# Front attention: a new order on TensorE, VectorE and ScalarE, and two more copies on VectorE

## What is computed

```python
    scores = jnp.einsum('bhid,bhjd->bhij', q, k)
    rel = jnp.einsum('bhid,pd->bhip', q, rel_key)
    rel_idx = jnp.clip(j - i + p - 1, 0, p - 1)
    bias = jnp.take_along_axis(rel, rel_idx, axis=3)
    logits = jnp.where(j <= i, (scores + bias) * scale, -jnp.inf)
    attn = jax.nn.softmax(logits, axis=-1)
    out = jnp.einsum('bhij,bhjd->bhid', attn, v)
    return out.transpose(0, 2, 1, 3).reshape(b, s, e) @ Wo + bo
```

## Time and profile before

| | |
|---|---|
| median of 3 runs | 4286.01 us (4283.55 to 4286.08) |
| span of the profiled execution | 4281.5 us, 4.5 us under the median |
| TensorE matmul busy | 4088.3 us (95%) |
| TensorE weight load busy | 2939.1 us (69%) |
| VectorE busy | 3495.0 us (82%) |
| ScalarE busy | 3716.8 us (87%) |
| GpSimd busy | 2399.2 us (56%) |
| DMA, share of 16 engines | 26.8% over the span, 0.74 in the front attention |

### The profile page before, as it was taken

One profiled execution on the slowest core, in us unless ns is written; L12 is line 12 of the kernel. 1 busy time (PEld: TensorE's weight loads), 2 busy tenths in 40 slices (PEclk: granted clock), 3 DMA queues, 4 the chain that ended last, 5 costly groups with the idle time before them and its releaser, 6 DMA issues. The chain is left out here.

```text
span 4281.5 us, 124222 instructions
## 1 busy us (share of the span) xinstructions
PE 4088.3 (95%) x43826; PEld 2939.1 (69%) x43826; DVE 3495.0 (82%) x8236; ACT 3716.8 (87%) x7186; POOL 2399.2 (56%) x2876
## 2 busy tenths in 40 slices
PE   4999999987999999999999999999999999999995
PEld 2566666654777777777777777777777777777774
DVE  4788888866888888888888888888888888888884
ACT  4899999966998989989999899998999989999895
POOL 4000000026667776777777777777777777767763
PEclk7999999988999999999999999999999999999997
DMA  6777777741111111111111111111111111111111
GB/s 180 229 230 228 235 226 237 224 142 35 44 42 42 47 36 44 42 42 47 37 43 43 42 47 37 41 45 42 47 37 43 43 42 47 37 43 42 42 47 52
DMA packets 249884, 347.65 MB, mean 81 GB/s; under 512 B 45120, under 2 KB 206508, under 8 KB 249260
## 3 DMA queue, kind: packets, MB, share of 16 engines
q1 hardware_dynamic: 249388, 341.00, 26.8%
HBM read 151.13 MB, written 82.85 MB: 55 GB/s over the span
## 5 line engine op out<-in xcount | busy, mean ns | idle before, releaser
L1468 PE MATMUL la_ps<-la_Wqkv,la_xsT 128*128 128x512 f32 x2304 | 1181.3, 608 | 5.5 <-DVE X L1173 5.5
L1173 DVE TENSOR_TENSOR X<-la_ps,la_tab 128x1024 f32<-128x1024 f32 x768 | 934.3, 1217 | 116.8 <-ACT la_sq L1317 107.7
L1120 POOL TENSOR_TENSOR la_rt<-la_rt,la_rn 128x1024 f32<-128x1024 f32 x384 | 722.4, 1902 | 27.5
L1103 POOL TENSOR_TENSOR la_rt<-X 128x512 f32<-128x512 f32 x384 | 494.7, 1288 | 319.1 <-PE la_ps L1483 243.3
L1505 PEld LDWEIGHTS la_ps<-la_kT,la_qB 128*64 128x64 f32 x12288 | 389.3, 138 | 230.2 <-issue 218.8
L1180 DVE TENSOR_REDUCE la_ssum<-la_sq 128x8 f32<-128x512 f32 x768 | 503.2, 676 | 0.0
L1104 POOL TENSOR_TENSOR la_rt<-X 128x512 f32<-128x512 f32 x384 | 497.3, 1295 | 0.0
L1317 ACT ACTIVATE la_sq<-la_ps 128x512 f32<-128x512 f32 x768 | 457.7, 596 | 15.5 <-PE la_ps L1468 5.4
L1468 PEld LDWEIGHTS la_ps<-la_Wqkv,la_xsT 128*128 128x128 f32 x2304 | 377.9, 191 | 132.9 <-issue 93.5
L526 POOL COPY at_vh<-V 128x64 f32 (+1 forms) x64 | 15.1, 236 | 784.3 <-PE at_ps L725 783.2
L1505 PE MATMUL la_ps<-la_kT,la_qB 128*64 128x64 f32 x12288 | 442.4, 225 | 0.2 <-ACT la_kT L1349 0.2
(11 more groups left out here) (207 smaller groups left out, 9544.0 us busy)
## 6 DMA issues: line engine op xcount, KB each, us to landing
at_band<-skew_scratch SPq DMA_DIRECT2D x64, 1536.0 KB, 7.3
la_vs<-la_v SPq DMA_DIRECT2D x192, 384.0 KB, 3.5
skew_scratch<-at_R SPq DMA_DIRECT2D x64, 1024.0 KB, 6.6
la_vs<-la_v SPq DMA_DIRECT2D x192, 128.0 KB, 3.4
la_Wqkv<-in_wqkv SPq DMA_DIRECT2D x28, 384.0 KB, 4.7
at_qh<-qt_scratch SPq DMA_DIRECT2D x64, 144.0 KB
at_kh<-kt_scratch SPq DMA_DIRECT2D x64, 144.0 KB
la_W<-in_L_ffn_W SPq DMA_DIRECT2D x24, 341.0 KB, 4.5
```

The lines of the kernel that those rows point to most:

```text
L1103: e.tensor_tensor(dst[:, :, 0, :], c[:, :, 0, :], s[:, :, 1, :], ALU.add)
L1120: e.tensor_tensor(heads(rt, w), heads(rt, w), wide(rn[:, w * H:(w + 1) * H], D), ALU.mult)\
L1173: e.tensor_tensor(dst.rearrange("p f (h d) -> p f h d", d=D), ps[:, c % 2, :].rearrange("p (h d) -> p h d", d=D).unsqueeze(1).to_broadcast ...
L1468: e.matmul(ps[:, c % 2, :], xsT[:, m * P:(m + 1) * P], Wqkv[:, ds(layer(n) % 2, 1), c * 512:(c + 1) * 512], start=True, stop=True)\
```

## The change

`BY_DVE` grows from (3, 6, 10) to (2, 3, 6, 8, 10): VectorE copies turned blocks 2 and 8 too, which ScalarE did. The bodies of the three engines are reordered. The steps themselves, their waits, and SyncE's and GpSimd's programs don't change. On TensorE turns, scores and values are mixed more finely; between rel(n, 0) and scores(7) of head n-3 now stand turn 8, turn 9, values 1 and turn 10 of head n-4, scores 6 of n-3, turn 11 of n-4, rel(n, 1) and turn 0 of n-3. scores 2 and 3, turn 4 and values 0 move from the end of a round to the start of the next. On VectorE far_least(4) and drain(0) go to the start of the next round, drain(1) goes behind minimum 7, and over_sum(1) behind minima 0 and 1 of the next head. On ScalarE the round begins with rel(0)'s copy.

```diff
--- before.py
+++ after.py
@@ -40,7 +40,7 @@
 QKV_Q = 3 * INNER // LOADS
 RING_V, RING_T = 4, 4
 DEEPEST = 7
-BY_DVE = (3, 6, 10)
+BY_DVE = (2, 3, 6, 8, 10)
 DEEPEST_A = 4
 
 
@@ -578,35 +578,41 @@
 
             def body(t):
                 for n, m in t.back(4):
+                    drain(n, m, 0)
                     copied(n, m, 6)
+                for n, m in t.back(3):
+                    far_least(n, m, 4)
+                    least(n, m, 4)
+                for n, m in t.back(4):
                     over_sum(n, m, 0)
                 for n, m in t.back(3):
-                    least(n, m, 4)
                     far_least(n, m, 5)
+                for n, m in t.back(4):
+                    copied(n, m, 8)
+                for n, m in t.back(3):
                     least(n, m, 5)
                 for n, m in t.back(4):
                     copied(n, m, 10)
                 for n, m in t.back(3):
                     far_least(n, m, 6)
                     least(n, m, 6)
-                for n, m in t.back(4):
-                    drain(n, m, 1)
-                for n, m in t.back(3):
                     far_least(n, m, 7)
                     least(n, m, 7)
                 for n, m in t.back(4):
+                    drain(n, m, 1)
+                for n, m in t.back(2):
+                    least(n, m, 0)
+                for n, m in t.back(3):
+                    copied(n, m, 2)
+                for n, m in t.back(2):
+                    least(n, m, 1)
+                for n, m in t.back(3):
+                    copied(n, m, 3)
+                for n, m in t.back(4):
                     over_sum(n, m, 1)
-                for n, m in t.back(3):
-                    copied(n, m, 3)
-                for n, m in t.back(2):
-                    least(n, m, 0)
-                    least(n, m, 1)
+                for n, m in t.back(2):
+                    far_least(n, m, 3)
                     least(n, m, 2)
-                    far_least(n, m, 3)
-                for n, m in t.back(3):
-                    drain(n, m, 0)
-                for n, m in t.back(2):
-                    far_least(n, m, 4)
                     least(n, m, 3)
             rounds(e, body, HEADS_A, RING_A, DEEPEST_A)
 
@@ -637,42 +643,41 @@
                 e.activation(dst, src, ACT.Copy).then_inc(tA.sem, 1)
 
             def body(t):
-                for n, m in t.back(3):
-                    exp(n, m, 3)
-                for n, m in t.back(4):
-                    copied(n, m, 8)
-                    copied(n, m, 9)
-                for n, m in t.back(3):
-                    exp(n, m, 4)
-                for n, m in t.back(4):
-                    copied(n, m, 11)
-                for n, m in t.back(3):
-                    exp(n, m, 5)
                 for n, m in t.back(0):
                     rel(n, m, 0)
-                for n, m in t.back(3):
-                    exp(n, m, 6)
-                    copied(n, m, 0)
-                    copied(n, m, 1)
+                for n, m in t.back(4):
+                    copied(n, m, 9)
+                for n, m in t.back(3):
+                    exp(n, m, 5)
+                for n, m in t.back(4):
+                    copied(n, m, 11)
                 for n, m in t.back(0):
                     rel(n, m, 1)
                 for n, m in t.back(3):
-                    copied(n, m, 2)
+                    copied(n, m, 0)
+                    exp(n, m, 6)
+                    copied(n, m, 1)
                     exp(n, m, 7)
                 for n, m in t.back(2):
                     exp(n, m, 0)
-                    exp(n, m, 1)
                 for n, m in t.back(0):
                     rel(n, m, 2)
+                for n, m in t.back(2):
+                    exp(n, m, 1)
                 for n, m in t.back(3):
                     copied(n, m, 4)
+                for n, m in t.back(2):
+                    exp(n, m, 2)
+                for n, m in t.back(3):
                     copied(n, m, 5)
                 for n, m in t.back(2):
-                    exp(n, m, 2)
+                    exp(n, m, 3)
                 for n, m in t.back(0):
                     rel(n, m, 3)
                 for n, m in t.back(3):
                     copied(n, m, 7)
+                for n, m in t.back(2):
+                    exp(n, m, 4)
             rounds(e, body, HEADS_A, RING_A, DEEPEST_A)
 
         @block.tensor
@@ -736,55 +741,54 @@
                 mm.then_inc(g_mm.sem, 1)
 
             def body(t):
-                for n, m in t.back(4):
+                for n, m in t.back(3):
+                    scores(n, m, 2)
+                    scores(n, m, 3)
+                for n, m in t.back(4):
+                    turn(n, m, 4)
                     turn(n, m, 5)
-                for n, m in t.back(3):
-                    scores(n, m, 4)
+                    values(n, m, 0)
+                    turn(n, m, 6)
                 for n, m in t.back(1):
                     rel(n, m, 3)
-                for n, m in t.back(4):
-                    turn(n, m, 6)
+                for n, m in t.back(3):
+                    scores(n, m, 4)
+                for n, m in t.back(4):
                     turn(n, m, 7)
                     gather(n, m, 0)
+                for n, m in t.back(3):
+                    scores(n, m, 5)
+                for n, m in t.back(0):
+                    rel(n, m, 0)
+                for n, m in t.back(4):
                     turn(n, m, 8)
                     turn(n, m, 9)
-                for n, m in t.back(3):
-                    scores(n, m, 5)
-                for n, m in t.back(4):
                     values(n, m, 1)
                     turn(n, m, 10)
+                for n, m in t.back(3):
+                    scores(n, m, 6)
+                for n, m in t.back(4):
                     turn(n, m, 11)
-                for n, m in t.back(3):
-                    scores(n, m, 6)
                 for n, m in t.back(0):
-                    rel(n, m, 0)
-                for n, m in t.back(4):
-                    values(n, m, 2)
+                    rel(n, m, 1)
                 for n, m in t.back(3):
                     turn(n, m, 0)
                     scores(n, m, 7)
-                for n, m in t.back(0):
-                    rel(n, m, 1)
-                for n, m in t.back(3):
                     turn(n, m, 1)
                 for n, m in t.back(4):
-                    gather(n, m, 1)
+                    values(n, m, 2)
                 for n, m in t.back(3):
                     turn(n, m, 2)
-                    turn(n, m, 3)
+                for n, m in t.back(2):
+                    scores(n, m, 0)
                 for n, m in t.back(0):
                     rel(n, m, 2)
-                for n, m in t.back(2):
-                    scores(n, m, 0)
+                for n, m in t.back(3):
+                    turn(n, m, 3)
+                for n, m in t.back(2):
                     scores(n, m, 1)
-                for n, m in t.back(3):
-                    values(n, m, 0)
-                for n, m in t.back(2):
-                    scores(n, m, 2)
-                for n, m in t.back(3):
-                    turn(n, m, 4)
-                for n, m in t.back(2):
-                    scores(n, m, 3)
+                for n, m in t.back(4):
+                    gather(n, m, 1)
             rounds(e, body, HEADS_A, RING_A, DEEPEST_A)
```

More of the change, by code:

```diff
@@ L597, in body @@
                 for n, m in t.back(4):
-                    over_sum(n, m, 1)
+                    drain(n, m, 1)
[5 more added lines that the diff above has]
+                    least(n, m, 1)
                 for n, m in t.back(3):
                     copied(n, m, 3)
+                for n, m in t.back(4):
+                    over_sum(n, m, 1)
                 for n, m in t.back(2):
-                    least(n, m, 0)
-                    least(n, m, 1)
+                    far_least(n, m, 3)
                     least(n, m, 2)
-                    far_least(n, m, 3)
-                for n, m in t.back(3):
-                    drain(n, m, 0)
-                for n, m in t.back(2):
-                    far_least(n, m, 4)
                     least(n, m, 3)
@@ L738, in body @@
             def body(t):
+                for n, m in t.back(3):
+                    scores(n, m, 2)
+                    scores(n, m, 3)
                 for n, m in t.back(4):
+                    turn(n, m, 4)
                     turn(n, m, 5)
+                    values(n, m, 0)
+                    turn(n, m, 6)
+                for n, m in t.back(1):
+                    rel(n, m, 3)
                 for n, m in t.back(3):
                     scores(n, m, 4)
-                for n, m in t.back(1):
-                    rel(n, m, 3)
                 for n, m in t.back(4):
-                    turn(n, m, 6)
                     turn(n, m, 7)
                     gather(n, m, 0)
-                    turn(n, m, 8)
```

(18 more changed lines are left out.)

## The result

The changed kernel takes 4526.14 us (median of 4 runs, 4506.09 to 4540.98) against 4284.78 us before in the same session. The ratio is 1.0561, 95% interval 1.0541 to 1.058: slower by 5.6%. The prediction said slower, by 129 us and at most 189; it is 241. The loop that it describes is there: where TensorE's clock stays up, heads come about 14.2 to 14.6 us apart, for 14.35 forecast. What the clock does in the loop was priced at 27 us, about a sixth of what it costs.

The account below looks back on a forecast made before the run. The prediction took a one-head loop through the DMA queue, tied with TensorE's work, as the bound. From 4286 us, +99 (loop) + 3 (end) + 27 (clock) = +129 gave 4415 us; range 4367 to 4475.

Parts of the forecast that it names:

- The loop that it describes: Front attention: rel(n,0), scores(7) three heads back, VectorE reductions, band load, q and k behind it, next rel(n,0); 14.35 us a head.
- What bounds the kernel now: Front attention before the change: the loop through the DMA queue and TensorE's own work tie, at 12.67 us a head.
- TensorE's order, 3.49 us, and VectorE's, 5.74: From rel(n,0)'s start: scores(7) starts after 3.49 us instead of 1.78; minimum 7 is read out after 5.74.
- Transfer part 8.5, loop 14.35: Band issue to next rel(n,0) takes 8.5 us; with band issue at 5.85, 14.35 a head against 12.67, +99 us.
- the clock stays: Rival: TensorE's clock stays at 2.4 GHz throughout, 4388 us; chance 0.25.
- The ring's order: DMA queue: descriptors are consumed in order, so q and k loads can't start before the band's; 6.85 us against 3.63.
- the loads are not held by the band load: Rival: q and k don't wait behind the band load, engines decide at 12.2 us a head, about 4261 us; chance 0.06.
- Skew write, start, end: Skew write not binding, about 2 us in hand; first loads unaffected; last rounds add 3 us (0 to 6).
- Turns spread between scores and values: TensorE's and ScalarE's short waits on each other go, but this counts for nothing while the loop binds.
- Clock: Pause of some 2 us before rel(n,0): a fall to half rate loses 1.7 us, in three heads of ten, 27 us.
- nearly every head: Rival: the clock falls in nearly every head, 90 us, about 4478 us in all; chance 0.13.
- Copies 2 and 8 lie beside TensorE's work: The copies add about 0.69 and 0.43 us to VectorE, 11.4 of 14.35 us, hidden beside TensorE's work.

Follow-up runs that it names:

- the first experiment: Changed kernel with SyncE issuing the q and k loads of head n+1 ahead of the band load of head n-1: 4266.22 us, ratio 0.9968.
- 8 fillers: Changed kernel with 8 unneeded matmuls added ahead of the wait for q and k of rel(n,0): 4408.11 us, ratio 1.0293.
- 16 fillers: Changed kernel with 16 unneeded matmuls added ahead of the wait for q and k of rel(n,0): 4391.7 us, ratio 1.0258.
- the run with three copies: Changed kernel with q and k loads ahead of the band load and copies 2 and 8 back on ScalarE: 4264.33 us, ratio 0.9961.

## Why the prediction was wrong

The step that failed is the one on the clock: the fall was priced at 1.7 us and given to three heads in ten. The runs show about 2.7 us in nearly every head. The other steps, one by one:

- *What bounds the kernel now*: right. The tie of loop and TensorE is shown by the run of the kernel before with the loads first, which gains 9 us, and by the first experiment.
- *TensorE's order, 3.49 us, and VectorE's, 5.74*: right. There are two heads early on in which the clock stayed at 1.00. In them R0 stands at 143.18 and 173.72, the band's issue 5.88 and 5.87 us behind (5.85 predicted), and the next R0 at 157.81 and 188.00 (PE's timeline, and SyncE's queue):

```profile
143.18 0.28 PE L694 MATMUL at_ps<-at_relD,at_qh 72*128 72x256 bf16 x1 [1.67 <-DMA at_kh<-kt_scratch]
...
157.81 0.28 PE L694 MATMUL at_ps<-at_relD,at_qh 72*128 72x256 bf16 x1 [1.94 <-DMA at_kh<-kt_scratch]
...
173.72 0.28 PE L694 MATMUL at_ps<-at_relD,at_qh 72*128 72x256 bf16 x1 [1.64 <-DMA at_kh<-kt_scratch]
...
188.00 0.28 PE L694 MATMUL at_ps<-at_relD,at_qh 72*128 72x256 bf16 x1 [1.59 <-DMA at_kh<-kt_scratch]
```

```profile
149.06 0.36 SPq L506 DMA_DIRECT2D at_band<-skew_scratch  x1
...
179.59 0.36 SPq L506 DMA_DIRECT2D at_band<-skew_scratch  x1
```

- *Transfer part 8.5, loop 14.35*: right, for heads without a fall. The transfer part is 8.75 and 8.41 us in those two heads, 8.32 and 8.42 in the two of the section above. The loop is 14.63 and 14.28 there and 14.18 in the mean with 8 fillers. The 4391.7 us with 16 fillers come close to the prediction's own case "the clock stays", 4388, in part by luck, since there TensorE's own work with the fillers takes 14.27 us and sets the distance.
- *The ring's order*: the step that has q and k held up by the band's load in front of them is borne out by the run with the wait kept and the load gone from in front. That the whole 8.3 us is the band's transfer is more than was shown. (The case "without it", which that step calls the first rival's, is the second of the list, "the loads are not held by the band load".)
- *Skew write, start, end*: right; band loads wait for the minima alone, and the last rounds cost 4 us in the profiled run where 3 were put.
- *Turns spread between scores and values gain nothing while the loop binds*: right. Without the loop the gain is 4 us, which the intervals can't tell from none, and not the 25 of the rival in which nothing holds the loads: TensorE's own instructions fill 12.5 us, not 12.2.
- *Clock*: this is the term that was mis-sized, twice. The size of one fall: I took 3.4 us at half rate, from the one stretch of the earlier trace rows. Here nearly all of the half-rate stretches are 6.8 us long, twice that. Windows of the changed kernel, the last one with one of the few that are shorter:

```profile
510.10:516.90 6.80, 5.68 (x24) 3.08 (x25) 2.38 (x7) 2.09 (x4) 0.00 (x0) 0.50 0.46 141
...
516.90:527.10 10.20, 9.63 (x74) 6.23 (x72) 8.63 (x35) 8.93 (x16) 0.24 (x1) 1.00 0.63 194
...
527.10:533.90 6.80, 5.86 (x25) 3.26 (x26) 2.63 (x7) 2.27 (x4) 0.00 (x0) 0.51 0.45 137
...
189.30:192.70 3.40, 3.40 (x16) 1.33 (x9) 1.70 (x6) 1.57 (x3) 0.00 (x0) 0.50 0.16 49
```

  The half-rate stretch begins in the pause, 0.9 us ahead of R0 at 528.04, and covers the 5.8 us behind it, so all of the loop's part on TensorE. R0 to band issue is 8.62 us instead of 5.88: 2.74 us a fall, not 1.7. For a stretch of 3.4 us the 1.7 was right: with 8 fillers a head with such a fall takes 15.9 us in the mean instead of 14.18. And the number of falls: I took three heads in ten, between "1.32 us did nothing" and "2.84 us lowered it". From head 9 (R0 at 204.02) to head 63 every head has one, all but two of them 6.8 us long; they begin 17.0 us apart (510.1, 527.1), as the heads do. 16.9 less 14.2 to 14.3 is 2.6 to 2.7 us for 59 heads, 154 to 159 us, where the forecast had 27 and its rival "nearly every head" 90. The runs with 16 and 8 fillers show that it is the idle pause: 134 and 118 us come back.
- *Copies 2 and 8 lie beside TensorE's work*: right for the new order, which the run with three copies shows. I gave the same reason for the old one when I laid out that run, and there it was wrong by 0.9 us a head: busy time left over on VectorE says nothing on whether a copy comes in time for the block that waits for it.

The range failed since its upper end, 4475, was made of that rival's price (and lay 3 us under the rival's own 4478), and the price was a single stretch from another part of the kernel. What stays open is what decides whether the clock falls. The pause's length alone does not: in the changed kernel the clock stayed at 1.00 behind pauses of 1.67 and 1.64 us (143.18, 173.72) and fell behind one of 1.59 (188.00; the window from 189.30 on). Nor is it known why a fall lasts 6.8 us here and 3.4 with 8 fillers. Gather(0) and scores(5) stand right ahead of this pause; what TensorE did in them was not varied.

## What to carry to other kernels

Before an order is changed on the engines, follow each resource that is loaded once a round back to what releases its issue, queue neighbours included: steps put between a load's first user and the step that lets the next load go are added to the period one for one. Put the small load that is needed first ahead of the large one in the queue; the swap was worth 260 us here. Put the queue right first, and judge an order of the engines after that: with the loads first, the old and the new orders here were within 5 us of each other. And a new pause on TensorE is to be priced with the clock: if it repeats each round, assume that it lowers the clock each round, and that the work right behind it, which is the loop's own, runs at half rate.

## What the hardware showed unexpectedly

Pauses of 1.3 to 2.0 us, one in every round of about 17 us, went with half-rate stretches of 6.8 us that begin inside the pause in the heads shown. Period and stretches settled at 17.0 us together, 2.8 us over the 14.2 that the loop takes at the full clock (the mean with 8 fillers). Pauses of about the same length early on (1.67 and 1.64 us) went with no fall, and pauses of 0.7 us with one in some heads. Sixteen matmuls whose result is thrown away, put into the pause, took 134 us off the kernel's time; elsewhere in the round they added 78.
